# Finer sums and an unbroken first quad in the second attention, and feed-forward tiles begun while the second batch is sorted

## What is computed

```python
def _L1_attn_ref(x, W_dq, W_uq, W_dkv, W_uk, W_uv, W_o):   # 16 heads of 8
    scores = jnp.einsum('bqhd,bkhd->bhqk', Q, K) / math.sqrt(D_K)
    scores = jnp.where(causal, scores, -jnp.inf)
    attn = jax.nn.softmax(scores, axis=-1)
    return jnp.einsum('bhqk,bkhd->bqhd', attn, V).reshape(Bx, Sx, N_HEADS * D_K) @ W_o
def _L1_ffn_ref(hidden_states, Wg, W1, W3, W2):            # 8 experts, the best 2 for each token
    top_g, top_i = jax.lax.top_k(jax.nn.softmax(x @ Wg, axis=-1), K)
    y = silu(x @ W1[e]) * (x @ W3[e]) @ W2[e]              # weighed by top_g and added
```

## Time and profile before

| | |
|---|---|
| median of 3 runs | 1022.32 us (1022.24 to 1022.61) |
| the profiled execution | 1022.52 us |
| its span | 1020.8 us |
| mean granted PE clock | 0.912 of full |
| busy: PE, DVE, ACT, POOL | 886.3, 727.2, 546.1, 434.0 us |

### The profile page before, as it was taken

How to read it: one execution, slowest core, us unless ns; L and a number is a source line. 1 busy time by engine, 2 the same in 40 slices (tenths; PEclk the granted TensorE clock), 3 DMA queues, 4 the chain that set the end, 5 groups by cost and what they waited for, 6 DMA issues and landing times.

```text
span 1020.8 us, 17889 instructions
## 1 busy us (share of the span) xinstructions
PE 886.3 (87%) x5819; PEld 425.7 (42%) x5826; DVE 727.2 (71%) x1548; ACT 546.1 (53%) x643; POOL 434.0 (43%) x825
## 2 busy tenths in 40 slices
PE   6699999999999977589993796999999999859992
PEld 4222232232232444369991543334343334346561
DVE  6779989989989768734444399687787866354446
ACT  4498898898898732212231510466565655723331
POOL 3154552552552550048883410233433343627762
PEclk9599999999999999879996658699999998969996
DMA  5301011011020131217754333822133015123123
GB/s 188 127 1 48 9 40 47 11 35 46 11 77 1 45 102 31 57 38 196 187 112 99 128 110 107 194 56 87 51 96 95 1 50 170 61 62 121 42 87 100
DMA packets 74061, 79.70 MB, mean 78 GB/s; under 512 B 14904, under 2 KB 60824, under 8 KB 70520
## 3 DMA queue, kind: packets, MB, share of 16 engines
q1 hardware_dynamic: 65008, 67.51, 22.0%
q0 software_dynamic: 8128, 9.84, 4.7%
q10 hardware_dynamic: 864, 1.57, 0.4%
HBM read 57.23 MB, written 21.68 MB: 77 GB/s over the span
## 4 chain that ended last, share of the span: by engine, by line
PE 54%; DVE 26%; issue 9%; POOL 5%; ACT 3%; DMA 2%; DVEq 1%; SPq 0%; ACTq 0%; POOLq 0%
PE acc_ps L838 10%; PE acc_ps L1202 7%; DVE mx L567 7%; PE tail_ps L1139 5%; PE causal_ps L1182 5%; PE causal_ps L1366 5%; DVE R L1734 4%; POOL moe_rows L2462 4%; DVE tails L1740 3%; PE causal_ps L800 3%; PE causal_ps L811 2%; PE tail_ps L1383 2%; POOL G L2453 1%; PE tail_ps L800 1%; DMA moe_rows<-out_e,idx 1%
## 5 line engine op out<-in xcount | busy, mean ns | idle before, releaser
L1611 ACT ACTIVATE EX<-causal_ps 128x1024 f32<-128x1024 f32 (+1 forms) x154 | 140.6, 939 | 140.9 <-PE causal_ps L1182 140.5
L567 DVE TENSOR_REDUCE mx<-tail_ps 128x1 f32<-128x512 f32 x266 | 158.2, 634 | 45.9 <-PE tail_ps L1142 33.2
L1469 ACT ACTIVATE R<-R 128x2048 f32<-128x2048 f32 (+1 forms) x80 | 134.7, 1737 | 0.5 <-DVE R L1734 0.5
L1139 PE MATMUL tail_ps<-KM,QM 72*128 72x512 bf16 (+1 forms) x320 | 106.7, 355 | 6.6 <-DVE mx L567 2.5
L2504 POOL TENSOR_TENSOR pacer<-eps_ln 128x1 f32<-128x1 f32 x140 | 27.4, 196 | 190.0 <-ACT EX L1611 189.2
L1734 DVE TENSOR_SCALAR R<-causal_ps 128x1024 f32<-128x1024 f32 (+1 forms) x88 | 94.1, 1071 | 14.9 <-PE causal_ps L800 13.8
L1740 DVE TENSOR_REDUCE tails<-causal_ps 128x1 f32<-128x768 f32 (+4 forms) x96 | 92.9, 968 | 10.6 <-PE causal_ps L811 9.8
L1476 ACT ACTIVATE R<-R 128x1792 f32<-128x1792 f32 (+4 forms) x80 | 100.5, 1268 | 0.0
L1182 PE MATMUL causal_ps<-QE,KE 75*128 75x512 bf16 (+3 forms) x369 | 99.4, 341 | 0.8 <-ACT EX L1611 0.5
L2347 POOL TENSOR_TENSOR R<-R 128x512 f32<-128x512 f32 (+2 forms) x64 | 87.3, 1381 | 1.3
L1202 PE MATMUL acc_ps<-EX,VS 128*32 128x512 f32 (+3 forms) x768 | 84.5, 516 | 0.9 <-DVE EX L2251 0.6
(11 more groups left out here) (397 smaller groups left out, 1693.8 us busy)
## 6 DMA issues: line engine op xcount, KB each, us to landing
QS<-q_parts SPq DMA_DIRECT2D x8, 576.0 KB
KS<-k_parts SPq DMA_DIRECT2D x24, 192.0 KB
QM<-q_parts SPq DMA_DIRECT2D x8, 576.0 KB
KM<-k_parts SPq DMA_DIRECT2D x24, 192.0 KB
QE<-q_parts SPq DMA_DIRECT2D x8, 576.0 KB
KE<-k_parts SPq DMA_DIRECT2D x24, 192.0 KB
wg<-in_wg_t SPq DMA_DIRECT2D x16, 256.0 KB, 2.9
wu<-in_wu_t SPq DMA_DIRECT2D x16, 256.0 KB, 3.2
```

The costliest lines, as they stand in the source:

```text
L567: return reduce(mx[:, par, hh, o0:o0 + step * (cnt - 1) + 1:step], scores[:, 0:cnt * w].rearrange("p (c w) -> p c w", w=w), AX.X, op, **how)
L1139: mm = pe.matmul(slot[:, at:at + w], QM[0:ROWS, par, hh, i * P:(i + 1) * P], KM[0:ROWS, par, hh, k0:k0 + w], start=True, stop=not diag, sk ...
L1469: act.activation(R4[:, rp, h0:h0 + 2, 0:width], R1[:, rp, h0:h0 + 2, 0:width], ACT.Square).then_inc(squared, 1)
L1611: act.activation(EX[:, rp, hh, 0:width], slot[:, 0:width], ACT.Exp, scale=float(D) ** -0.5).then_inc(exp_done, 1)
```

## The change

`sum_cuts` cuts the sums of key tiles 1 to 7 at multiples of 256: eighteen groups a quad instead of twelve, with the same columns, and their weight in `among` is 4 per column. Quad 0 begins when the banks of its first two scores are reduced; first jobs 78 and 79 stand behind those scores, in `tail_ps`, and the gathering, turning and splitting of quad 1's maxima move into quad 0, at the places that they have in all quads. In the feed-forward, tiles 0 to 6 of batch 0 are interleaved with the sorting of batch 1; `take_sorted` moves from DVE to ACT, `weigh_slots(1)` from POOL to DVE, and POOL scatters four tiles, then sends batch 1, then scatters the rest. The core of the diff (in the rows after it, the changed kernel's line numbers are 17 to 24 higher for the same operation):

```diff
@@ -83 +83 @@
     return [(kt, at + qa - kt * P, qa, qb) for kt, at, n in pieces(s)[0] for qa, qb in cut(kt * P, T, 0)]
+def sum_cuts(s):
+    out = []
+    for kt, at, n in pieces(s)[0]:
+        first = kt * P
+        edges = [0, BANK, T] if kt == 0 else [first] + [q for q in range(0, T + 1, BANK // 2) if q > first]
+        out += [(kt, at + qa - first, qa, qb) for qa, qb in zip(edges, edges[1:])]
+    return out
@@ -174 +184 @@
+LAST_FIRST = [(i, 4 + i - 2 * len(MAX) + 2) for i in range(2 * len(MAX) - 2, 2 * len(MAX))]
+BANK_OF = {i: i % 6 for i in range(2 * len(MAX) - 2)} | dict(LAST_FIRST)
@@ -183 +197 @@
 TE = KT * E1
+EARLY_TILES = 4
@@ -1146 +1163 @@
                 at_least(pe, max_done, len(MAX) * (g - 2) + n - 1)
-                if n == TURNED_AT and not first:
+                if first and n < 2:
+                    pe.wait_ge(first_max, 2 * len(MAX) - 1 + n)
+                if n == TURNED_AT:
                     turn_max(g - 1)
-                if n == TURNED_AT + 2 and not first:
+                if n == TURNED_AT + 2:
...
                 i += len(MAX) * g
-                at_least(pe, first_max, i - 5)
-                row_scores(banks[i % 6], g, i % len(MAX)).then_inc(first_full, 1)
+                at_least(pe, first_max, i - 5 if i < LAST_FIRST[0][0] else i - 1)
+                row_scores(banks[BANK_OF[i]], g, i % len(MAX)).then_inc(first_full, 1)
@@ -1174 +1193 @@
                     if n == 0:
+                        if isinstance(g, int) and g == 0 and nth < 2:
+                            pe.wait_ge(first_max, 2 * len(MAX) - 6 + 2 * nth)
@@ -1186 +1207 @@
             def exp_sums(g, par, s):
-                rp, cuts = (par + s) % 2, value_cuts(s)
+                rp, cuts = (par + s) % 2, sum_cuts(s)
...
                     if k == 0:
+                        if isinstance(g, int) and g == 0 and s == 0:
+                            pe.wait_ge(m_sb, 1)
@@ -1201 +1224 @@
                                        EX[:, rp, hh, c0:c0 + qb - qa], start=(kt == 0),
-                                       stop=(kt == STEPS[-2 if qb <= BANK else -1][0]), tile_position=(0, hh * VW))
+                                       stop=(kt, qb) in ((STEPS[-2][0], BANK), (STEPS[-1][0], T)), tile_position=(0, hh * VW))
...
                         mm.then_inc(exp_summed, 1)
-                return [(2 * (qb - qa), lambda k=k: group(k)) for k, (_, _, qa, qb) in enumerate(cuts)]
+                return [(4 * (qb - qa), lambda k=k: group(k)) for k, (_, _, qa, qb) in enumerate(cuts)]
@@ -1248 +1271 @@
                                   start=True, stop=True)
-                    first_job(g, i)
-            pe.wait_ge(first_max, 2 * len(MAX))
+                    if g * len(MAX) + i < LAST_FIRST[0][0]:
+                        first_job(g, i)
@@ -1303 +1325 @@
                     pe.wait_ge(max_in[par], 16 * STACK_DMAS * (k + 2))
+                if not with_max and turn_maxima:
+                    turn_max(g + 1)
                 if first:
-                    turn_max(1, acc_ps)
-                    pe.wait_ge(m_sb, 2)
-                elif not with_max and turn_maxima:
-                    turn_max(g + 1)
-                jobs = [cut for hh in range(2) for cut in exp_scores(g, par, 0, hh)]
+                    for hh in range(2):
+                        run_all(exp_scores(g, par, 0, hh))
+                        first_job(1, LAST_FIRST[hh][0] - len(MAX))
+                    jobs = []
+                else:
+                    jobs = [cut for hh in range(2) for cut in exp_scores(g, par, 0, hh)]
@@ -1397 +1421 @@
             second_half = {(0, 0): [lambda: run_all(turn_exp(NQ - 1)), lambda: turn_half(1, (6, 7)),
-                                    lambda: route_half(1, 6), project_third, lambda: count_half(1, 6), project_fourth,
-                                    lambda: total_experts(1, 6), lambda: place(1, 6)]}
+                                    lambda: route_half(1, 6)],
+                           (0, 1): [lambda: count_half(1, 6), project_third],
+                           (1, 1): [lambda: total_experts(1, 6)],
+                           (2, 1): [lambda: place(1, 6), project_fourth]}
@@ -1656 +1682 @@
-            second_half = {0: [lambda: exp_evacuate(NQ - 1), lambda: copy_yt(1, 2, 6), lambda: copy_yt(1, 3, 7),
-                               lambda: gate_tanh(1), lambda: standardise_rows(2), lambda: standardise_rows(3)]}
+            def take_sorted(b, i):
...
+                act.activation(ST[:, s % 2, 0:n], banks[5][:, 0:n], ACT.Copy).then_inc(xt_sb, 1)
+            second_half = {0: [lambda: exp_evacuate(NQ - 1), lambda: copy_yt(1, 2, 6), lambda: copy_yt(1, 3, 7)],
+                           6: [lambda: gate_tanh(1), lambda: standardise_rows(2)],
+                           7: [lambda: standardise_rows(3)]}
...
                 if q < NL:
+                    b, j = divmod(q, LT)
+                    if j == 0:
+                        take_sorted(b, 0)
+                    if j % CT == 2 and j // CT + 1 < NG:
+                        take_sorted(b, j // CT + 1)
@@ -2084 +2126 @@
                 dve.wait_ge(first_full, i + 1)
-                maxima(g, n, banks[i % 6], dve.tensor_reduce, ALU.max, negate=True).then_inc(first_max, 1)
+                maxima(g, n, banks[BANK_OF[i]], dve.tensor_reduce, ALU.max, negate=True).then_inc(first_max, 1)
@@ -2092 +2134 @@
                     parts_of_max(0, acc_ps)
-            gather_max(1, 1)
-            parts_of_max(1, acc_ps)
...
                     row_max_of(g + 2, par, n)
-                    if n == 0 and not first:
+                    if n == 0:
...
                         exp_normalise(g - 1)
-                    if n == TURNED_AT and not first:
+                    if n == TURNED_AT:
@@ -2214 +2254 @@
-            def take_sorted(b, i):
...
+            def weigh_slots(b):
+                dve.wait_ge(weights[b], 16 * (3 * E0 // 4 + 1))
+                dve.wait_ge(weights[2 + b], 16 * (3 * E0 // 4 + 2))
+                dve.wait_ge(f_weighed, b)
+                link(dve.tensor_tensor(chosen[:, :, :, :],
...
+                link(dve.tensor_reduce(w_slot[:, b, :, :], chosen[:, :, :, :], AX.X, ALU.add))
+                dve.tensor_copy(to_row[:, b * LT:(b + 1) * LT], w_slot[:, b, 1, :]).then_inc(f_weighed, 1)
@@ -2274 +2315 @@
-            def sum_second(n):
...
             second_half = {0: [lambda: exp_normalise(NQ - 1), lambda: gate_logits(1, 6), lambda: gate_ranks(1),
-                               lambda: sum_second(2), lambda: take_counts(1, 6), lambda: sum_second(3),
-                               lambda: pad_experts(1, 6), lambda: gate_gap(1), lambda: reciprocal_roots(1),
-                               lambda: gate_scale(1), lambda: take_slots(1, 6), lambda: gate_weights(1)]}
+                               lambda: take_counts(1, 6)],
+                           1: [lambda: residual(1, 2, 7), lambda: pad_experts(1, 6)],
+                           2: [lambda: moments(2, 2), lambda: gate_gap(1)],
+                           3: [lambda: residual(1, 3, 7), lambda: take_slots(1, 6)],
+                           4: [lambda: moments(2, 3)],
+                           5: [lambda: reciprocal_roots(1), lambda: gate_scale(1)],
+                           6: [lambda: gate_weights(1)],
+                           LT + 1: [lambda: weigh_slots(1)]}
...
                 if q < NL:
-                    b, j = divmod(q, LT)
-                    if j == 0:
-                        take_sorted(b, 0)
-                    if j % CT == 2 and j // CT + 1 < NG:
-                        take_sorted(b, j // CT + 1)
@@ -2541 +2577 @@
-            pool.wait_ge(zeros_out, 16 * (1 + 2 * B))
-            for b in range(B):
+            def send_rows(b):
@@ -2550 +2586 @@
                                                     ap=to_slot[:, b, c * KT + t:c * KT + t + 1].bitcast(U32), axis=0)).then_inc(f_sent[b], 16)
-                if b == 0:
-                    weigh_slots(0)
-            for q in range(NL):
-                if q == 6:
-                    weigh_slots(1)
+            def scatter_tile(q):
...
                                         ).then_inc(scattered[q // LT], 16)
+            pool.wait_ge(zeros_out, 16 * (1 + 2 * B))
+            send_rows(0)
+            weigh_slots(0)
+            for q in range(EARLY_TILES):
+                scatter_tile(q)
+            send_rows(1)
+            for q in range(EARLY_TILES, NL):
+                scatter_tile(q)
```

17 lines of the change are left out of this document (8 added, 9 removed).

## The result

The changed kernel took **1015.49 us** (median of 4 runs, 1014.84 to 1017.84) against 1022.28 for the kernel before in the same session: ratio 0.9942, 95% interval 0.9919 to 0.9965. The forecast was 1013.0, its range 1006 to 1018.5. So it gains 4 to 7 us, and the sign and the range were right. The parts behind that figure were not all right, as the stages show.

What follows compares the result with a forecast made beforehand. PE was taken to bound steady quads and the tiles, at slow clock in quad 0, with a DVE chain behind the attention. 1022.5 + 1.4 - 4.2 - 6.4 = 1013.3, stated as 1013.0 us, range 1006 to 1018.5.

Steps and rivals of the forecast that it cites:

- Part 1: Attention quads: finer sums add PE work but recover waits for DVE; net +1.4 us, between -7 and +9.
- The count of close pairs: Loop body of two quads: neighbouring job pairs with less PE work than DVE's 1.2 us fall from 31 of 79 to 10.
- 1.3 to 2.8: Steady quad: us that PE was reckoned to wait, from 30.9 of work in 32.2.
- Part 2: First quad: job 8 begins 4.6 us earlier, less 0.4; -4.2 us, between -2.7 and -8.5.
- the 0.4 for the split: Quad 0: 0.4 us taken off the gain because splitting the maxima stops the maximum jobs once.
- Rival 1: Quad 0: PE's clock stays up, gaining 6.5 to 8.5 us instead of 4.2; 1009.5 us; chance 0.22.
- The rule on idleness: PE's clock gate, from the Trainium skill: it throttles after idleness and sustained work releases it.
- Part 3: Feed-forward: batch 0's tiles no longer wait for batch 1, tile 9 comes earlier; -6.4 us, between -3 and -9.
- The gain that I had counted from the clock: Feed-forward: dense tiles from 900 on should bring PE's full clock back sooner; counted within the -6.4 us.
- 2: Feed-forward: POOL becomes its end, gain 4.1, or about 3 with a wait at tile 23; 1016 us; chance 0.18.
- 3: Attention: 48 added groups of sums cost more than their columns show, kernel slower from 0.22 a group; 1026 us; chance 0.04.
- 4: Whole change: early tiles stall on DVE, clock falls at once, sums cost +5; 1022 us; chance 0.06.

Runs made afterwards that it cites:

- E2: Changed kernel with the twelve old groups of sums but the new weight of 4 per column: 1011.0 us, ratio 0.9877.
- E6: Changed kernel with its eighteen new groups of sums at the old weight of 2 per column: 1015.39 us, ratio 0.9920.
- E1: Changed kernel with the twelve old groups of sums and their old weight of 2: 1006.57 us, ratio 0.9863.
- E9: E1 with weight 4 outside quads 6 and 7, and filling matmuls in quad 0's first step and behind the attention: 1003.35 us, ratio 0.9826.
- E10: E9 plus a filling matmul over 256 columns ahead of sixteen score tiles in quad 6: 1004.23 us, ratio 0.9831.
- E7: E1 plus a 384-column filling matmul behind each of nine maximum jobs in quad 0's first step: 1006.47 us, ratio 0.9832.
- E4: Changed kernel with the old feed-forward order behind the attention on PE, ACT, DVE and POOL: 1022.92 us, ratio 0.9999.
- E5: The changed kernel again, unchanged, in a later session: 1018.31 us (12 runs), ratio 0.9955.
- E3: Changed kernel with the old beginning of quad 0, all first maxima done before it: 1020.0 us, ratio 0.9978.
- E8: Changed kernel with the weighing of batch 1's slots back on POOL, ahead of the fourteenth scatter: 1021.16 us, ratio 0.9977.
- E11: Changed kernel with fourteen small unused additions on POOL ahead of the thirtieth scatter: 1021.19 us, ratio 0.9991.

## Why the prediction was right or wrong

**Part 1, finer sums (+1.4, bounds -7 to +9): the step that failed.** The first half of the step held: "+1.0 us of PE per quad" was 1.0 (9.5 to 10.5 for the groups in quad 3). The second half, "I take 1.2 us back per quad in quads 1 to 5", measured 0.4 in quads 1 to 4, and over the five quads about half of what I took. Quads 1 to 5 became 1.9 us slower in all (162.2 to 164.1) and not 1 us faster, 32.8 for quad 3, where I had said 31.6 to 32.4.

The count of close pairs was a fair guide to the waits for DVE, which fell from 20 to 9. But those are waits of the weight loads, and PE's matmuls stood idle for only 1.05 us in the quad, not for "1.3 to 2.8". My sum had put the groups at 11.3 where they take 9.5 from start to start, and the rest at 19.6 where it takes 22.7 with all its waits; what I called waiting was partly work. In the changed kernel PE is idle for 1.10: the pauses for DVE's maxima are mostly gone, and pauses for the exponential (0.32 and 0.27) and for the split of the maxima (0.32) stand there. These new pauses are not the cause of the loss, though: E2 has them and its quads are shorter than before, E6 has none of that length and its quad 3 is 0.45 longer than before. What costs is the groups, with too little idle time in the quad to pay for them.

The other three quads came to 2.5, where I had 2.4: quad 7 to the last sum +1.2 (I said +0.4), quad 6 at full clock 28.84 to 29.56, +0.7 (+1.0), quad 0 +0.6 (+1). Together **+4.4**. My upper bound of +9 was more than its own terms give (5 + 2.4). That the groups and not the weight cost it, E2 and E6 show.

**Part 2, the first quad (-4.2, bounds -2.7 to -8.5): right in mechanism, too small.** The 4.6 us up to job 8 came as computed, and the clock fell near 640, as said (641.0). I then let "the rest of the quad run as before", with an unchanged rest at half clock. Behind job 8 it was at half clock for 6.8 us and not for the 12.5 of before (644.35 to 656.9), so the rest took 29.6 us instead of 31.3 although its sums were finer, and the 0.4 for the split was not needed: PE was busy throughout those 6.8 us, in which the split lies. Together **-7.0** (87.8 to 80.8 with the old sums, E1). Rival 1 gave the same size but for another reason; the clock did not stay up. When it is made to (E9, against E2), quad 0 takes 33.98 instead of 36.15, another 2.2.

The trace has PE idle for 1.11, 0.35 and 0.21 us, and never longer, between 632 and 641, and the clock falls. The Trainium skill ("TensorE: Matmul & The Clock Gate", the section on a second HAM failure mode, psum-queue depth-cycling) says that frequent micro-idles between groups of matmuls, as a kernel cycles through PSUM banks, are enough for the gate to swing between half and full. The trace agrees with it: these waits are for banks that DVE must free. In E9 and E10 matmuls stand between them and the fall is gone, although the pause of 1.11 is still there; in E7, without the two behind the first jobs 78 and 79, the fall came sooner and was short. Which of the waits brings it is not shown. The rule on idleness that I had cited did not cover it.

**Part 3, the feed-forward (-6.4, bounds -3 to -9): right.** 33.7 to 27.4 us from the logits to tile 9 at equal clock in the logits (before and E1), **-6.3**; E4 and E5 give 6.4. Tile 9 came 27.6 behind the logits (I had said about 27). The sends began at 925.39 and not at 923, and POOL kept up with 0.6 to 1.3 us to spare (1.7 forecast). Tile 23's wait of 1.42 is no new cost: before it was 1.51, and tile 9 to tile 45 takes 66.4 before and 66.5 after. The gain that I had counted from the clock did not show: PE was at half clock from 893.5 to 907.2 in the changed kernel.

**The sum.** +4.4 - 7.0 - 6.3 = -8.9, where I had -9.2. Two misses of 3 us, in parts 1 and 2, offset each other, which is luck. The measured medians lie 4 to 7 below before, so 2 to 5 are still to be explained. By the profiles 3.2 to 3.5 of them are the clock behind quad 5: the two profiles of the changed kernel lost 4.1 and 5.3 us in quad 6 and 1.3 to 2.2 in the logits, that of before 3.1 and nothing. That I had not priced at all. The new sums seem to make a fall likelier. The profiles alone are too few: five of the seven with the new sums had both losses (E3 only that in the logits, E6 only that in quad 6), and of the four with the old sums and no filling there (before, E1, E2, E7) only E2; quad 6 alone fell in six of seven and in three of four. But the runs have a mean clock each. Of the kernels with the new first quad and feed-forward and no filling behind quad 0, 11 of the 17 runs with the old sums (E1, E2, E7) had 0.924 or more, and 3 of the 46 with the new sums (the first session, E5, E6, E8, E11). The time of E1, 8 to 9 us below the changed kernel's where the stages of part 1 explain 4.4, points the same way. If so, the finer sums cost about 4 us on top of the +4.4; why they would bring the fall stays open.

**Rivals.** 1: its clock stays up in no profile of the changed kernel. 2: not there, E11 shows what it would look like. 3: the groups cost 0.12 (E6) to 0.17 each and not 0.22, and the kernel is faster, but part 1 by itself was the loss that this rival named. 4: no.

**A better kernel.** With the old sums, the new first quad, the new feed-forward and the fillings (E9) the time is 1003.35 us, 1.7% below before and 12 to 15 us below the changed kernel. Most of that is the old sums: E1, with nothing filled, is at 1006.57.

## What to carry to other kernels

Before counting the waits that an interleaving removes, look whose waits they are. Here 10.5 us of waits stood on the weight loads and only 1.05 us of idle time on the matmuls, and about half of the expected gain did not come. Only the matmuls' idle time can be won, and a removed pause can come back as a wait for the next holder of a buffer. Compare traces stage by stage between the same instructions: where the clock differs from execution to execution, whole times hide terms of a few us that the stages show to 0.1. And where a short stretch is paced by a slower engine, filling TensorE's waits with a harmless matmul into a free bank can be worth something on top of the rearrangement: here 2.2 us behind the 7.0.

## What the runs showed of the hardware

The granted clock is not tied to the code alone: kernels with the same quad 6 ran it at full clock in one execution (28.84 us) and partly at half in another (34.65, E7), without an idle stretch of note before the fall (20.41 us busy of the 22.15 before it in the changed kernel). With PE's pauses filled it came back to 2.4 GHz before 639 in the middle of a DVE-paced step (E7), and stayed there from the first jobs to the end of the quad (1.00 in E9 and E10).

Cutting groups of sums smaller costs 0.12 to 0.17 us of PE for each further group, with the same columns streamed (0.7 us in E6 and 1.0 in the changed kernel for six more groups in quad 3).

The weight loads' waits are mostly hidden behind running matmuls: 10.5 us of waiting for DVE in a quad in which PE was idle for 1.05 (before, quad 3).
